# A transformer layer on one core: the weight-split stores and the output store change places in the sync queue

## The reference

```python
q = proj(query, Wk, bk); k = proj(key, Wk, bk); v = proj(values, Wv, bv)
scores = q @ k.T / sqrt(dk)                                  # strictly causal (mask = 1)
p = softmax(where(allow, scores, NEG)) * allow
dist = sqrt(clip((sum(p) - cumsum(p)) * abs(i - j), 0))
effect = clip(exp(-softplus(gamma) * dist), 1e-5, 1e5)
attn = softmax(where(allow, scores * effect, NEG))
x = layer_norm(query + (attn @ v) @ Wo.T + bo)
out = layer_norm(x + relu(x @ W1.T + b1) @ W2.T + b2)
```

## Time and profile before

| | us |
|---|---|
| median of three runs | 1758.15 |
| lowest, highest | 1756.3, 1767.09 |
| the profiled execution | 1767.09 |
| its span (first to last instruction) | 1765.0 |
| mean granted TensorE clock, share of 2.4 GHz | 0.943 |
| PE busy | 1543.5 (87%) |
| DVE busy | 1143.2 (65%) |
| ACT busy | 1032.7 (59%) |
| POOL busy | 142.4 (8%) |

### The profile page before, as it was taken

One profiled execution on the slowest core, in us unless ns is written; L12 is line 12 of the kernel. 1 busy time (PEld: TensorE's weight loads), 2 busy tenths in 40 slices (PEclk: granted clock), 3 DMA queues, 4 the chain that ended last, 5 costly groups with the idle time before them and its releaser, 6 DMA issues.

```text
span 1765.0 us, 36811 instructions
## 1 busy us (share of the span) xinstructions
PE 1543.5 (87%) x13056; PEld 1268.6 (72%) x13056; DVE 1143.2 (65%) x3828; ACT 1032.7 (59%) x2674; POOL 142.4 (8%) x107
## 2 busy tenths in 40 slices
PE   4566799998999999899999999899999999887875
PEld 3454587886877777787877777787878787666664
DVE  6778966768675777668675776667676776632221
ACT  1586766656666666666666666566666666642111
POOL 7333100001010000001010000001010000000000
PEclk9786899999999999999999999999999999998888
DMA  5654254665565565556565565556556564656664
GB/s 185 223 178 181 107 168 167 208 197 182 199 207 181 179 204 182 191 181 215 191 203 181 174 209 172 192 185 198 189 204 204 181 203 157 205 202 219 221 213 143
DMA packets 81244, 334.55 MB, mean 190 GB/s; under 512 B 10256, under 2 KB 10256, under 8 KB 64272
## 3 DMA queue, kind: packets, MB, share of 16 engines
q1 hardware_dynamic: 81040, 331.92, 55.4%
HBM read 306.72 MB, written 25.17 MB: 188 GB/s over the span
## 4 chain that ended last, share of the span: by engine, by line
PE 69%; DVE 13%; ACT 11%; issue 5%; POOL 1%; ACTq 0%; DVEq 0%; POOLq 0%
PE bank L200 20%; PE bank L201 17%; PE bank L202 17%; PE bank L380 6%; PE bank L394 4%; DVE w_sb L913 3%; DVE w_sb L925 3%; ACT h_sb L715 3%; DVE h_lo L1002 3%; ACT h_hi L721 2%; PE bank L414 2%; PE bank L404 2%; ACT w_sb L643 1%; ACT w_sb L645 1%; ACT p_sb L656 1%
## 5 line engine op out<-in xcount | busy, mean ns | idle before, releaser
L1002 DVE TENSOR_TENSOR h_lo<-h_sb,h_hi 128x512 fp32r<-128x512 f32 x128 | 102.5, 801 | 379.8 <-ACT h_hi L721 379.8
L200 PE MATMUL bank<-xt_hi,w_ring 128*128 128x256 f32 x1024 | 298.7, 292 | 13.6 <-DVE xt_lo L996 8.2
L201 PE MATMUL bank<-xt_lo,w_ring 128*128 128x256 f32 x1024 | 290.4, 284 | 9.8 <-issue 9.8
L202 PE MATMUL bank<-xt_hi,w_ring 128*128 128x256 f32 x1024 | 290.4, 284 | 0.0
L200 PE MATMUL bank<-w_ring,h_hi 128*128 128x512 f32 x512 | 226.0, 441 | 60.6 <-DVE h_lo L1002 60.6
L715 ACT ACTIVATE h_sb<-bank,b_col 128x256 f32<-128x256 f32 x256 | 106.7, 467 | 259.0 <-PE bank L202 259.0
L200 PEld LDWEIGHTS bank<-xt_hi,w_ring 128*128 128x128 f32 x1024 | 196.6, 192 | 27.0 <-issue 18.2
L665 ACT COPY pt_sb<-bank 128x512 f32<-128x512 f32 x192 | 111.3, 580 | 178.7 <-PE bank L394 178.7
L201 PE MATMUL bank<-w_ring,h_hi 128*128 128x512 f32 x512 | 212.6, 415 | 0.0
L202 PE MATMUL bank<-w_ring,h_lo 128*128 128x512 f32 x512 | 212.0, 414 | 0.0
L656 ACT ACTIVATE p_sb<-w_sb,nm 128x32 f32<-128x32 f32 (+7 forms) x512 | 206.0, 408 | 0.0
(11 more groups left out here) (120 smaller groups left out, 3018.2 us busy)
## 6 DMA issues: line engine op xcount, KB each, us to landing
w_ring<-w_split SPq DMA_DIRECT2D x128, 1024.0 KB, 4.9
w_ring<-w_split SPq DMA_DIRECT2D x256, 512.0 KB, 3.8
w_split<-w_ring SPq DMA_DIRECT2D x32, 512.0 KB, 4.2
x_raw<-x_t SPq DMA_DIRECT2D x16, 512.0 KB, 3.7
c_raw<-ctx_t SPq DMA_DIRECT2D x16, 512.0 KB, 4.4
u_sb<-x_rows SPq DMA_DIRECT2D x16, 512.0 KB, 5.5
ring_raw<-w SPq DMA_DIRECT2D x32, 256.0 KB, 3.1
out<-rows SPq DMA_DIRECT2D x16, 512.0 KB, 6.1
```

The source lines that it names most:

```text
L200: nc.tensor.matmul(dst, a_hi, b_hi, start=start, stop=False)
L201: nc.tensor.matmul(dst, a_hi, b_lo, start=False, stop=False)
L202: return nc.tensor.matmul(dst, a_lo, b_hi, start=False, stop=stop)
L1002: nc.vector.tensor_tensor(h_lo[:], h_sb[:], h_hi[:].bitcast(F32), ALU.subtract).then_inc(h_lo_ok, 1)
```

## The change

Two pieces of SP's program move. Nothing else changes: the same DMAs are issued with the same waits, and no other engine's program is touched.

- The output store leaves its place in c = 0, between the weight loads of pair 2 and pair 3, and stands at the end of c = 1, behind the weight loads of pair 5. In the last step, 19, it moves from c = 0 to c = 1, with nothing in between.
- The stores of the split weights, and the raw loads that follow them, come one quarter earlier in SP's order: tiles 0 and 1 at c = 0 of step 0 (before: c = 1), tiles 14 and 15 at c = 3 of step 1 (before: c = 0 of step 2). So tiles 2 and 3, and in step 1 tiles 10 and 11, now stand ahead of that step's `x_in` and `c_in`, where they stood behind them.

```diff
-            def rows_out(i, slot):
-                sp.wait_ge(out_ok, RT * (i - 4) + RT)
-                alone(sp)
-                sp.dma_start(out_by_batch[i - 4], rows[:, slot]).then_inc(out_st, 16)
...
-                    if isinstance(i, int) and 1 <= NQ * i + c <= NP:
-
-                        for f in (8 * i + 2 * c - 2, 8 * i + 2 * c - 1):
+                    if isinstance(i, int) and i < 2:
+                        for f in (8 * i + 2 * c, 8 * i + 2 * c + 1):
                             store_hidden(f)
                             if f + 3 < FT:
                                 raw_hidden(f + 3)
...
-                    if c == 0 and done and not ffn:
-                        rows_out(i, slot)
                     if older if c == 3 else ffn:
                         for p in ps:
-                            if c == 0 and done and p == ps[1]:
-                                rows_out(i, slot)
                             g = NP * b + p
...
                                     w2_tile((2 * p + 2 + r) % FT)
+                    if c == 1 and done:
+                        sp.wait_ge(out_ok, RT * (i - 4) + RT)
+                        alone(sp)
+                        sp.dma_start(out_by_batch[i - 4], rows[:, slot]).then_inc(out_st, 16)
```

## The result

The changed kernel takes 1813.97 us (median of four runs, 1810.75 to 1817.18) against 1758.61 for the kernel before (four runs beside it): a ratio of 1.0314, with a 95% interval of 1.0254 to 1.0372. It is 55.4 us slower, 3.1%. The forecast was 1817 us, slower.

The account below looks back on a forecast made before the run. The prediction took PE to set the pace in the steady steps. Stalls 28.5, step 17's 3, clock 18 and start 9 sum to 58.5 us, added to the median 1758.15 for 1817 us, range 1788 to 1852.

Parts of the forecast that it names:

- The store's way: Step 8, SP's queue: store goes out 2.07 us after pair 5's tile loads, lands 6.1 later, `shift1` 5.1 us late.
- The chain behind it: DVE from `shift1` through scan and scalings to `hidden_low` of pair 6: 4.25 us of delay arrive, with no slack between.
- The stall, 28.5: PE at `add_hidden` of pair 6, steps 4 to 15: twelve delays of 4.25 us less 22.5 of slack, 28.5 us.
- Step 17: Late store makes `shift1` and `hidden_low` end later than PE had started there: 3 us.
- step 16: `hidden_low` had idled 3.29 us for ACT and PE itself waits for ACT: counted 0, bounds 0 to 1.8.
- The clock, 18: PE in steps 4 to 15: one more low-clock stretch a step, 1.5 us each, 18 us.
- stall without the clock: Rival: PE's second idle time brings no low stretch of its own; 40 us lost, 1798 us, chance 0.17.
- The start, 9: Steps 0 and 1: `x_in` and `c_in` queue behind split stores and raw loads, `c_lo` and masks later; 9 us.
- Hidden: Rival: DVE's idle time or a quick landing hides the store's wait, only the start is lost; 1767 us, chance 0.07.
- Faster: Rival: earlier split stores let the first two steps run ahead, some 17 us; 1741 us, chance 0.03.
- Two low stretches a step: Rival: two low-clock stretches in each of twelve steps, 36 us, with landings of 7.0; 1853 us, chance 0.18.

Follow-up runs that it names:

- `out_inputs`: Only the output store moved, behind `x_in` and `c_in`, later than the change does, against the kernel before: 1841.97 us, ratio 1.050.
- `out_pair4`: Only the output store moved, behind the tile loads of pair 4 and ahead of those of pair 5, against the kernel before: 1760.90 us, ratio 1.0028.
- `att6_before`: The kernel before with six 128x512 matmuls ahead of attend in steps 4 to 15: 1750.09 us against 1761.18, ratio 0.9935.
- the two filled kernels: Kernel before and changed kernel, each with six matmuls ahead of attend, the changed one also eight ahead of `add_hidden`: 1750.09 and 1799.86 us.
- `out_alone`: Only the output store moved as in the change, split stores left in place, against the kernel before: 1795.17 us against 1754.76, ratio 1.0233.
- `late_before`: The kernel before with `shift1` moved on DVE behind `hidden_low` of pair 6: 1755.24 us against 1755.69, ratio 0.9997.
- `split_alone`: Only the split stores moved a quarter earlier as in the change, output store left in place, against the kernel before: 1770.51 us, ratio 1.0086.
- `act_inputs`: The kernel before with split stores moved as in the change, and ACT issuing `x_in` and `c_in` in steps 0 and 1: 1758.30 us, ratio 1.0016.
- `shift_late`: The changed kernel with `shift1` moved on DVE behind `hidden_low` of pair 6: 1768.34 us against 1754.76 for the kernel before, ratio 1.007.

## Why the prediction was right, and where its sum was not

**The store's way, right to a tenth.** It passes the loads of three pairs, 3 to 5 (the forecast's "four DMA groups" is a miscount on which nothing rests). Forecast: behind the tile loads of pair 5, 2.07 us after them; landing 6.1 us after its issue; `shift1` 5.1 us late. Measured: 810.44 - 808.38 = 2.06; `shift1` 5.97 after the issue; 112.7 / 14 = 8.05 us of idle time where there were 2.93, 5.1 late. The tile view's landings of the stores are as before (2.8 at the least, 6.1 in the median):

```profile
DMA to landing us min/median/max: 2.8/6.1/6.6
```

The fit of the Trainium skill (DMA: Bandwidth & Descriptors, "Anatomy of one DMA"), weighed in the forecast, gave an estimate of 3.2 us for this store; the page gives it for DMAs that GpSimd issues, and this one is issued by SyncE. The traces disagree by 2.9 in the median; only the last store, with nothing around it, is near it (2.8). The Trainium skill's advice in "Rules for kernel authors" of the same page, to issue early and wait late, agrees with `out_inputs`; `out_pair4` shows that a later issue costs nothing as long as it lands before its waiter comes.

**The chain behind it, right in kind, 0.7 too long.** Forecast: 4.25 us reach `hidden_low`, none recovered. From the start of `shift1` to the end of `hidden_low` it was 801.27 - 791.27 = 10.0 us before and is 824.84 - 816.41 = 8.43 after. Of the 1.57 less, 0.88 is the scan's idle time, which the forecast took off; 0.7 is new. It comes from the scalings, 0.9 shorter, while the small steps ahead of them are 0.3 longer. In the trace of before they (L925) lie beside both of POOL's input casts (L1167, and the next at 798.26):

```profile
796.73 3.94 DVE L925 SCALAR_TENSOR_TENSOR w_sb<-w_sb,gz,dist 128x160 f32<-128x160 f32 x8
...
797.02 1.04 POOL L1167 CAST x_hi<-x_raw 128x1024 fp32r<-128x1024 f32 x1 [76.12 <-DMA x_raw<-x_t]
```

After, they take 3.04 us. The casts start at 819.16 and 821.09, so the first lies beside the scan and only the second beside the scalings. The late chain leaves part of a collision behind, and 4.25 - 0.7 = 3.55 us are left of the delay at the end of `hidden_low`.

**The stall, 28.5: mis-sized.** The slacks read one by one were right as readings: 0.65 us in step 8, 2.2 in step 4. The step that failed is the sum of them. The 22.5 us of slack are large where the attend ahead ran at low clock (3.66 us instead of 2.19); there the stall is partly hidden behind a slow attend that itself already costs. At full clock the slack in step 8 is 0.65 and the stall 3.55 - 0.65 = 2.9. In `att6_before`, where no attend of the twelve steps is slow, the slack is 0.5 to 0.7 in eleven of them and 2.1 in step 15, 8.9 in all, which would leave 12 * 3.55 - 8.9 = 33.7; the two filled kernels differ by 35.4. Step 17 adds 2.2 (PE's wait there went from 2.30 to 4.51; 3 was forecast), step 16 nothing, as forecast. That is 37.6 us of the 40.4 that `out_alone` costs. The 2.8 between stay open; the interval of the 40.4 is wider than that (34 to 48).

**The clock, 18: largely counted twice.** A low stretch right behind `add_hidden` of pair 6 is there (the window of 0.50 above), as forecast, but in five of the twelve steps of that trace, not in all, and the clock of the changed kernel is lower, 0.935 against 0.948 for before beside it. Forecast for the twelve steps were 28.5 + 18 = 46.5 us; they lose 35 both unfilled and filled. In the kernel as it runs, the stall that the trace shows is smaller than forecast and not larger: PE's waits for `hidden_low` grew by 21.9 us where about 30 were forecast, and eleven of the twelve attends were slow (nine before), which hides a part. Of the 35.2 between `late_before` and `out_alone`, 22.7 lie between attend and `add_hidden` and 12.5 elsewhere. In the filled pair, with no attend slow, 32.6 of the 35.4 lie there (59.0 against 26.4): the loss is nearly all stall. So a stall read at mixed clock and a low stretch for each step can't both be charged in full. That one makes up for the other step by step is inferred from these sums; what is shown is that the sum stays the same. The rival "stall without the clock" had the mechanism closer (28.5 + 3 for the store, no clock) and the size too low.

**The start, 9: mechanism right, too small.** Forecast: `x_in` at 71.2, `c_lo` starting at 78.5, masks 5.7 later. Measured: 68.63, 78.50, and 82.63 against 76.95, 5.7 later. The load was issued 2.6 us sooner than forecast (SP needed 11.0 us for the two tiles, not 12.8, from 57.67 on) but took 6.3 us to land, where it took 4.0 before. DVE's `x_lo` now waits for POOL's `x_hi`, and `c_lo` starts behind it just when forecast; that it fits to the tenth is luck:

```profile
76.55 2.03 DVE L858 TENSOR_TENSOR x_lo<-x_raw,x_hi 128x1024 fp32r<-128x1024 f32 x1 [7.06 <-POOL x_hi L1161]
```

The trace of before was about 1.7 us later at this point than other executions with the old start (the row stands at 76.95 there and at 75.22 in `out_alone`), which the forecast could not see from one profile. Against `out_alone`, `split_alone` loses 7.5 in step 0 and 3.7 in step 1, and 2.2 more follow up to the `turn_rows` of step 2, 13.4 in all. The medians say 15.8 (interval 10.5 to 19.7), near the bound of 16 that was given; the 2.4 us between are inside that interval and not placed.

**The sum.** 28.5 + 3 + 18 + 9 = 58.5 against 55.4 measured. By the runs it is 35.4 + 2.2 + 2.8 (open) for the store, at full clock, and 15.8 for the start. The total is right partly by luck, because terms erred against each other: the start was 7 too small, the stall and the clock together 11 too large (taken at full clock, the stall 7 too small and the clock 18 too large).

**The rivals.** "Hidden" falls with the 112.7 us at L984 and PE's longer waits behind them. "Faster" falls with `split_alone`: the earlier split stores gain nothing even in `act_inputs`, where their harm is removed (1.0016). "Two low stretches a step" would need 36 us of clock beside the stall, and the store costs 40.4 in all; the longest landing was 6.6 us, not 7.0 throughout.

## What to carry to other kernels

Before a DMA is moved down its queue, find the first instruction that waits for it and read what stands behind that instruction on its in-order engine: here the 380 us that DVE idled ahead of `hidden_low` in all were worth nothing in this place: between `shift1` and `hidden_low` of pair 6 it idled for only 0.88 us a step. A wait costs its length less the slack of the chain behind it, and that slack must be read in steps that run at full clock, or the loss is counted once as a stall and again as clock. If the DMA has to be late, move its waiter behind the urgent work instead, which cost nothing here and took the whole stall away.

## What the runs showed of the hardware

- **Low clock followed idle times of about 2.2 us on PE in many steps, and matmuls that do nothing win a part back.** In the trace of before, nine of the twelve attends behind such an idle time ran at the lower clock for a part or all of their time, three did not; in `att6_before` none did. There, six 128x512 matmuls ahead of the attend in steps 4 to 15 lengthen PE's work there by 1.63 us and leave 0.84 of the idle time (the timeline of `att6_before` below). The kernel as a whole is 0.65% faster (ratio 0.9935, interval 0.9906 to 0.9965), the lowest ratio here, at a granted clock of 0.954 against 0.948. Nine do no better than six (0.9963, 0.9941 to 0.9984).

```profile
791.60 1.63 PE L556 MATMUL bank<-wv_hi,wk_hi 128*128 128x512 f32 x6
...
794.07 0.69 PE L404 MATMUL bank<-zi_wide,head_ones 128*128 128x256 f32 x2 [0.84 <-ACT pt_sb L670]
```

- **A cast on POOL slows DVE beside it.** The eight scalings took 2.32 us with no cast beside them (`shift_late`, and 2.32 or 2.33 in each of the 49 such groups of the trace of before), 3.04 with one beside them (after), and 3.94 with both casts beside them (before). The Trainium skill (GPSIMD Engine Reference, "Specifications") says that POOL shares its SBUF interfaces with VectorE and that DVE instructions with two SBUF inputs contend with it; the traces agree, and the size here is up to 1.6 us on 2.3.
- **A store ahead of a load delays the load.** In steps 4 to 14 `x_in` landed 3.6 us after its issue in the median before and 5.8 after, with the 512 KB store about 2.8 us ahead of it. In steps 2 and 3 of after, with no store ahead, it took 3.7 and 3.8.
